# A hybrid attention and feed-forward block on one core: its opening staged by halves

## The chip, the core and the metric

The kernel runs on one core of a Trainium2 chip. The metric is the device time of one execution in microseconds (us). A profiled execution is shown beside three timed ones. Engines are named as the profile names them: PE is TensorE, DVE is VectorE, ACT is ScalarE, POOL is GpSimd, SP is SyncE. SP's queue of DMA instructions is SPq.

## The reference

For eight batches of 1024 tokens of width 256 (all float32):

```python
xn = layernorm(x)                                  # no gain, no bias
h  = silu(xn @ W1 + b1);  u, v, q, k = split(h, 4) # W1 is 256 x 1024
s  = silu(q_h @ k_h.T) / 1024                      # 16 heads of width 16
y  = (layernorm(concat(s @ v_h) * u) * gamma + beta) @ W2 + b2
f  = layernorm(xn) * ln1_g + ln1_b
f  = gelu(f @ ternary(w1).T + fb1)                 # hidden width 1024
f  = (layernorm(f) * ln2_g + ln2_b) @ ternary(w2).T + fb2
out = x + y + f
```

`ternary(w)` scales w by the mean of its absolute values, rounds to -1, 0 or 1 and scales back. That mean needs a sum over all of w before the first ternary weight exists.

## The kernel before

Tokens of a batch are laid out as 128 partitions by 8 tiles (T = 8) of 256 columns. Products that need more than the matmul's own precision are split: an operand is written as a rounded high part plus the rest as a low part, and three passes (high by high, high by low, low by high) are added up. So `W1h` and `W1l` are W1's parts, `xp` holds the two parts of the normalized and transposed x, and `kst` and `qst` hold two parts each of k and q.

The attention scores use heads in pairs with stacked parts: k and q parts are written from `kst` and `qst` to scratch in HBM (`write_parts`) and read back into `KS` and `QS` in a stacked layout (`load_k`, `load_q`). A transfer of one half h (512 tokens) and one parity o of the pairs has its own semaphore. PE's `scores(b, g)` waits for them; group g = 0 needs half 0 and o = 0 of both, g = 4 needs half 1 of `KS`.

Every engine walks the same list of steps. A step's name is `kind.args`: `ln1` (moments of x), `xn.i` (normalize the tile pair i), `xt.i` (PE transposes it, ACT writes the high part, DVE the low part), `k.c.h`, `q.c.h`, `v.i`, `u.c.h` (projections; ACT applies silu for k and q, DVE adds the bias for v), `vs.c` (ACT puts silu(v) into `V`), and those of the feed-forward part. Steps that go through PSUM take turns on the two banks of `fill`: the next step on a bank waits until the one before has been evacuated.

The list `OPENING` is what runs before the first scores, for batch 0. Each engine adds its own work around it. These are the places that the change touches or that the steps below speak of:

- SP (L475 to L490): loads x as one DMA, then `w1raw`, the two biases `b1s` and `bvb` (semaphore `s_b1`, full at 32), the feed-forward weights `wfraw` and `wsraw`, and small vectors. Then, for each half h: write k parts, write q parts, and for o = 0, 1 `load_k` and `load_q`.
- POOL (L500 to L546): constants and the identity, `input_rstd` (add eps, power -0.5, then the ratio of two such powers), and the zero fill of `V` (L546, 3072 columns).
- DVE (L891 to L899): moments of x, both parts of W1 whole (`split_w1`), a wait for `s_b1`, and the rest of `OPENING`.
- ACT (L625 to L634): the wait for `s_b1`, the list, and after each `q` step one sum of absolute values (`sum_of_abs`, L622), of `wfraw` after `q.0.0` and of `wsraw` after `q.0.1`. For k.0.1 it first waits until the first k parts have been written to HBM, for q.0.1 until the first q parts have.
- PE (L1088 to L1095): 36 warm-up matmuls, `xt.0`, `xt.1`, 8 warm-up matmuls, then `k.0.0` after `s_w1s`.

After the opening, the first rounds of scores carry the setup (`setup_step`): a total of the absolute sums on PE (L1047), scales and broadcasts and ternary weights on DVE (L669 to L695), products with them on PE (L1053 to L1069) and the folded biases on DVE (L701 to L711). Each engine takes its instructions in order, so a round of scores behind such a product waits for it.

## Time and profile before

| | |
|---|---|
| median of three executions | 1508.13 us (1507.6 to 1510.3) |
| the profiled execution | 1508.56 us, its span 1506.8 us |
| mean granted clock of the profiled execution | 0.994 |
| PE busy | 1465.9 us (97%) |
| ACT busy | 1205.8 us (80%) |
| DVE busy | 898.0 us (60%) |
| POOL busy | 97.4 us (6%) |
| first scores matmul starts | 39.73 us into the span |

The span is counted from the first to the last record of the execution; the execution's own time is 1.76 us longer. A time of day in the text below is one of the span. In a timeline row, the first figure is when a run of like instructions starts, the second how long it lasts, and the bracket how long the engine had been idle and who released it. A group of matmuls in full precision (f32) shows as two records for each instruction.

### The profile page before, as it was taken

What the parts mean: (1) busy time and instruction counts of PE and PEld (TensorE: products, weight loads), DVE (VectorE), ACT (ScalarE), POOL (GpSimd) and SP (SyncE); (2) the same over time, 40 slices, a digit from 0 to 9 for tenths busy, and PEclk for the clock granted to TensorE, in tenths of its full rate; (3) what the DMA queues carried; (4) which work ended last, traced back from release to release, by engine and by line L of the source; (5) the groups of instructions that cost most, each with busy time, mean ns of one, the idle gap of its engine ahead of it and who ended that gap; (6) DMA issues with size and microseconds to landing.
All of it is one profiled execution on the core that took longest, in us unless ns stands there. A gap on an engine that the chain in (4) does not pass through costs nothing.

```text
span 1506.8 us, 25898 instructions
## 1 busy us (share of the span) xinstructions
PE 1465.9 (97%) x9914; PEld 783.7 (52%) x9914; DVE 898.0 (60%) x1716; ACT 1205.8 (80%) x1269; POOL 97.4 (6%) x193
## 2 busy tenths in 40 slices
PE   7899999999999999999999999999999999999997
PEld 6354555455554555555555545545555455554544
DVE  5537664576555765458654685547765576555654
ACT  2688788888888887888878878788788888888884
POOL 2000100010000100001000010000100001000000
PEclk9899999999999999999999999999999999999999
DMA  6442043510524105241063401443033510425100
GB/s 202 110 128 69 1 102 96 140 57 16 126 68 129 57 15 154 76 103 47 17 167 89 122 1 54 129 128 83 1 94 103 140 57 15 119 66 138 29 1 29
DMA packets 67436, 123.49 MB, mean 82 GB/s; under 512 B 12784, under 2 KB 14448, under 8 KB 66288
## 3 DMA queue, kind: packets, MB, share of 16 engines
q1 hardware_dynamic: 67312, 121.83, 29.6%
q8 instruction: 79, 1.29, 0.4%
q14 instruction: 45, 0.37, 0.1%
HBM read 79.84 MB, written 41.94 MB: 81 GB/s over the span
## 4 chain that ended last, share of the span: by engine, by line
issue 93%; POOLq 6%; POOL 1%; DVE 0%; DVEq 0%
POOLq L534 3%; POOL rs L520 1%; POOLq L510 1%; POOLq L526 1%; POOLq L519 0%; POOLq L528 0%; POOLq L524 0%; POOLq L522 0%; POOLq L219 0%; DVE part L772 0%; DVEq L219 0%; POOL ident L500 0%; POOL rat L529 0%; POOLq L504 0%; POOLq L503 0%
## 5 line engine op out<-in xcount | busy, mean ns | idle before, releaser
L562 ACT ACTIVATE attn<-scores 128x1024 f32<-128x1024 f32 x1024 | 991.3, 1023 | 228.4 <-PE scores L930 224.3
L949 PE MATMUL outs<-attn,V 128*32 128x512 f32 x4096 | 494.3, 600 | 0.0
L930 PE MATMUL scores<-QS,KS 64*128 64x512 f32 x2048 | 389.1, 453 | 13.0 <-ACT attn L562 7.5
L930 PEld LDWEIGHTS scores<-QS,KS 64*128 64x128 f32 x2048 | 163.1, 185 | 306.2 <-ACT attn L562 241.5
L949 PEld LDWEIGHTS outs<-attn,V 128*32 128x32 f32 x4096 | 107.2, 109 | 235.7 <-issue 235.6
L822 DVE TENSOR_TENSOR tmp<-fill,l2g 128x512 f32<-128x512 f32 x128 | 88.5, 692 | 89.8 <-PE fill L1014 81.8
L805 DVE SCALAR_TENSOR_TENSOR hid<-fill,ratq,fb1b 128x512 f32<-128x512 f32 x128 | 96.1, 751 | 77.0 <-PE fill L1005 72.1
L1021 PE MATMUL fill<-Wq,hgh 128*128 128x256 f32 x512 | 130.2, 292 | 1.8 <-DVE hgl L829 1.1
L987 PE MATMUL fill<-xp,W1h 128*128 128x512 f32 x384 | 128.2, 415 | 0.0
L1021 PE MATMUL fill<-Wq,hgl 128*128 128x256 f32 x512 | 124.9, 282 | 0.0
L1021 PEld LDWEIGHTS fill<-Wq,hgh 128*128 128x128 f32 x512 | 97.3, 190 | 19.0 <-issue 14.9
L1021 PEld LDWEIGHTS fill<-Wq,hgl 128*128 128x128 f32 x512 | 97.6, 191 | 0.6
L509 POOL TENSOR_TENSOR rp<-mv,epst 128x2 f32<-128x2 f32 x64 | 12.5, 195 | 1316.4 <-DVE mv L722 911.2
L829 DVE TENSOR_TENSOR hgl<-tmp,hgh 128x512 fp32r<-128x512 f32 x128 | 88.6, 692 | 10.1 <-issue 0.4
L987 PEld LDWEIGHTS fill<-xp,W1h 128*128 128x128 f32 x384 | 66.1, 188 | 35.7 <-issue 25.6
L1014 PE MATMUL fill<-ident,hid 128*128 128x128 f32 x512 | 78.4, 281 | 3.5 <-DVE hid L805 2.1
L718 DVE BATCH_NORM_STATS2 st<-hid 128x6 f32<-128x512 f32 x128 | 79.1, 681 | 3.3 <-issue 0.5
L987 PE MATMUL fill<-xp,W1l 128*128 128x512 f32 x192 | 75.2, 392 | 0.0
L1014 PEld LDWEIGHTS fill<-ident,hid 128*128 128x128 f32 x512 | 56.0, 141 | 35.4 <-issue 25.7
L1005 PE MATMUL fill<-Wq,yT 128*128 128x512 f32 x256 | 71.6, 408 | 1.0
L1005 PE MATMUL fill<-Wq,yX 128*128 128x512 f32 x256 | 72.0, 410 | 0.0
L607 ACT ACTIVATE hid<-hid 128x2048 f32<-128x2048 f32 x32 | 60.4, 1911 | 7.7 <-DVE hid L805 7.5
(112 smaller groups left out, 1339.0 us busy)
## 6 DMA issues: line engine op xcount, KB each, us to landing
QS<-q_scratch SPq DMA_DIRECT2D x256, 128.0 KB, 3.2
k_scratch<-kst SPq DMA_DIRECT2D x64, 256.0 KB
q_scratch<-qst SPq DMA_DIRECT2D x64, 256.0 KB
KS<-k_scratch SPq DMA_DIRECT2D x128, 128.0 KB, 3.2
KS<-k_scratch SPq DMA_DIRECT2D x256, 64.0 KB, 3.4
xin<-in_x SPq DMA_DIRECT2D x8, 1024.0 KB, 5.0
out_dram<-part SPq DMA_DIRECT2D x16, 512.0 KB, 2.7
w1raw<-in_W SPq DMA_DIRECT2D x1, 1024.0 KB, 7.2
```

Source lines behind the costliest of these rows:

```text
L562: nc.scalar.activation(attn_of(g)[:, 2 * hf:2 * hf + 2, :], SP[:, 2 * hf:2 * hf + 2, :], ACT.Silu).then_inc(s_silu, 1)
L607: nc.scalar.activation(rows, rows, ACT.Gelu).then_inc(s_gelu, 1)
L718: V_.bn_stats(st[:, j, n, :] if len(views) > 1 else st[:, j, :], v)
L805: V_.scalar_tensor_tensor(out=hid_of(t)[:, cols], in0=FP[:, k, :], scalar=ratq[:, t:t + 1], in1=fb1b[:, cols], op0=ALU.mult, op1=ALU.add). ...
L822: V_.tensor_tensor(tmp[:, :].rearrange("p (c n) -> p c n", n=P), FP[:, k, :].rearrange("p (c n) -> p c n", n=P), l2g[:, 4 * r:4 * r + 4].u ...
L829: V_.tensor_tensor(hgl[:, r, :], tmp[:, :], hgh[:, r, :].bitcast(F32), ALU.subtract).then_inc(s_hg, 1)
L930: ins = mm(SP[:, j, :], KS[rows, pair, t * P:(t + 1) * P], QS[rows, pair - c * PPC, h * HALF:(h + 1) * HALF], start=True, stop=True)
L949: ins = mm(OP[32 * j:32 * j + 32, g // RUN % 2, :], V[:, t, c * HPC // 2 + j, o * DH:o * DH + 2 * DH], attn_of(g)[:, n, :], start=(o == 0 ...
L987: ins = mm(bank.rearrange("p (i n) -> p i n", i=2), w[:, kc, col:col + P], xp[:, 2 * h:2 * h + 2, part, kc, :], start=n == 0, stop=n == le ...
L1005: ins = mm(bank, y_of(t // 2)[:, part, kc, t % 2 * P:(t % 2 + 1) * P], Wq1[:, kc, hf * HALF:(hf + 1) * HALF], start=n == 0, stop=n == len( ...
L1014: ins = nc.tensor.transpose(bank[:, n * P:(n + 1) * P], hid_of(t)[:, col:col + P], ident[:, :])
L1021: ins = mm(bank[:, 0:D], w[:, r, n * P:(n + 1) * P], Wq2[:, 4 * r + n, :], start=i == 0, stop=i == len(passes) - 1)
```

## The change

x is loaded by two DMAs of four tiles each. For batch 0 the moments and the rstd are computed for four tiles at a time, with POOL's first power made on constants ahead of any data. `ln1` is now run inside the loop over `OPENING`, and so behind the wait for `s_b1`. The tile pair 1 of batch 0 is normalized into `tmp` instead of `normed`, so that it need not wait for the transposes of pair 0. W1 is split in four instructions instead of two: the high part of the columns of q and k after `xn.1`, their low part after `xt.1`, the high part of the columns of u and v after `xn.2`, their low part after `q.0.0`; `v.0` waits for that last one. `xt.1` and `xt.2` move ahead of `xn.2` and `xn.3`. The first 36 warm-up matmuls become 26. The load of QS for half 0 and o = 0 is issued by ACT, after `xt.3`, and no longer by SP; `sum_of_abs(0)` moves from behind `q.0.0` to behind `v.1`, which is ahead of `k.0.1`.

```diff
-WARM = (36, 8)
+WARM = (26, 8)
...
-OPENING = parsed("ln1 xn.0 xn.1 xt.0 xn.2 xt.1 k.0.0 q.0.0 xn.3 xt.2 v.0 xt.3 v.1 k.0.1 q.0.1 v.2 v.3 vs.0")
+OPENING = parsed("ln1 xn.0 xn.1 xt.0 xt.1 xn.2 k.0.0 q.0.0 xt.2 xn.3 v.0 xt.3 v.1 k.0.1 q.0.1 v.2 v.3 vs.0")
...
+        def normed_of(x, i):
+            return tmp[:, :].rearrange("p (j n) -> p j n", j=2) if (x, i) == (0, 1) else normed[:, :, :]
...
             def load_x(b):
-                sp.dma_start(xin[:, :, :], xv[b, :, :, :]).then_inc(s_x, 16)
+                for ts in (slice(0, T // 2), slice(T // 2, T)) if b == 0 else (slice(0, T),):
+                    sp.dma_start(xin[:, ts, :], xv[b, :, ts, :]).then_inc(s_x, 16)
...
                     load_k(0, 0, h, o)
-                    load_q(0, 0, h, o)
+                    if h or o:
+                        load_q(0, 0, h, o)
...
+            nc.gpsimd.tensor_tensor(rs1[:, 0:T // 2], epst[:, 0:T // 2], mhalf[:, 0:T // 2], ALU.pow)
...
+                for hf in range(2) if b == 0 else ():
+                    ts = slice(hf * T // 2, (hf + 1) * T // 2)
+                    pool.wait_ge(s_mv1, hf + 1)
+                    nc.gpsimd.tensor_tensor(rp1[:, ts], mv1[:, ts, 1], epst[:, ts], ALU.add)
+                    pool.drain()
+                    nc.gpsimd.tensor_tensor(rs1[:, ts], rp1[:, ts], mhalf[:, ts], ALU.pow).then_inc(s_rs1, 1)
...
+            def load_first_q():
+                act.wait_ge(s_qw, WROTE)
+                qv = qd[0].rearrange("(e w) r n -> e r w n", e=2)
+                for e in range(2):
+                    for at_row in (0, QROWS):
+                        act.dma_start(QS[e * TERMS + at_row:e * TERMS + at_row + QROWS, 0::2, 0:HALF].bitcast(F32),
+                                      qv[e, :, 0::2, 0:HALF]).then_inc(s_qst[0][0], 16)
...
                 step(0, *s)
-                if s[0] == "q":
-                    sum_of_abs(s[2])
+                if s == ("xt", NP - 1):
+                    load_first_q()
+                if s in (("v", 1), ("q", 0, 1)):
+                    sum_of_abs(int(s[0] == "q"))
...
-            step(0, "ln1")
-            split_w1(False)
-            dve.drain()
-            split_w1(True)
             dve.wait_ge(s_b1, 32)
             for s in OPENING:
-                if s != ("ln1",):
-                    step(0, *s)
+                step(0, *s)
+                if s == ("xn", 1):
+                    split_w1(0, 1)
+                elif s == ("xt", 1):
+                    split_w1(1, 1)
+                elif s == ("xn", 2):
+                    split_w1(0, 0)
+                elif s == ("q", 0, 0):
+                    split_w1(1, 0)
...
-                if s == [s for s in OPENING if s[0] in ("k", "q", "v")][0]:
+                if s == ("k", 0, 0):
                     warm_up(WARM[1])
                     pe.wait_ge(s_w1s, 1)
+                elif s == ("v", 0):
+                    pe.wait_ge(s_w1s, 2)
```

The order of instructions at two places of the opening follows, with the semaphores that each row waits for (`x_loaded` is `s_x`, `projection_biases_loaded` is `s_b1`, `w1_loaded` is `s_w1`, `input_rstd` is `s_rs1`; `filled` and `evacuated` are the two banks, `q_parts_written` is `s_qw`). DVE at the start of the program, before:

```order
L718 BN_STATS st_88<-xin 128x6 [waits x_loaded]
L718 BN_STATS st_88<-xin 128x6 x7
L722 BN_AGGR mv_89<-st_88 128x2 x8
L647 CAST W1h<-w1raw 128x2048 [waits w1_loaded]
L649 TENSOR_TENSOR W1l<-w1raw,W1h 128x2048
L732 TENSOR_SCALAR normed<-xin,mv_89,rs_91 128x256 [waits projection_biases_loaded,input_rstd]
L732 TENSOR_SCALAR normed<-xin,mv_89,rs_91 128x256
L732 TENSOR_SCALAR normed<-xin,mv_89,rs_91 128x256 [waits filled0]
```

The same place of the changed program:

```order
L746 BN_STATS st_88<-xin 128x6 [waits projection_biases_loaded,x_loaded]
L746 BN_STATS st_88<-xin 128x6 x3
L750 BN_AGGR mv_89<-st_88 128x2 x4
L746 BN_STATS st_88<-xin 128x6 [waits x_loaded]
L746 BN_STATS st_88<-xin 128x6 x3
L750 BN_AGGR mv_89<-st_88 128x2 x4
L760 TENSOR_SCALAR normed<-xin,mv_89,rs_91 128x256 [waits input_rstd]
L760 TENSOR_SCALAR normed<-xin,mv_89,rs_91 128x256
L760 TENSOR_SCALAR tmp<-xin,mv_89,rs_91 128x256 x2
L674 CAST W1h<-w1raw 128x2x512 [waits w1_loaded]
L882 TENSOR_TENSOR xp<-fill,xp 128x512 [waits x_high_part] x2
L677 TENSOR_TENSOR W1l<-w1raw,W1h 128x2x512
```

The wait for the biases has moved from the first normalization to the first statistics, W1's split from ahead of the normalizations to behind them, and both low parts of xp now stand ahead of pair 2. ACT from its first q step to the values for the first scores, before:

```order
L568 ACTIVATE qst<-fill,b1s 128x512 [waits filled1]
L622 ACTIVATE junk,asum<-wfraw 128x2048 [waits wf_loaded]
L588 ACTIVATE xp<-fill 128x512 [waits filled0] x2
L568 ACTIVATE kst<-fill,b1s 128x512 [waits filled0,k_parts_written]
L568 ACTIVATE qst<-fill,b1s 128x512 [waits filled1,q_parts_written]
L622 ACTIVATE junk,asum<-wsraw 128x2048 [waits abs_summed,ws_loaded]
L580 ACTIVATE V<-vraw 128x8x4x16 [waits evacuated1,pool_constants]
```

And now:

```order
L583 ACTIVATE qst<-fill,b1s 128x512 [waits filled1]
L603 ACTIVATE xp<-fill 128x512 [waits filled0] x2
L646 DMA QS<-q_scratch 32x2x512 [waits q_parts_written]
L646 DMA QS<-q_scratch 32x2x512 x3
L637 ACTIVATE junk,asum<-wfraw 128x2048 [waits wf_loaded]
L583 ACTIVATE kst<-fill,b1s 128x512 [waits filled0,k_parts_written]
L583 ACTIVATE qst<-fill,b1s 128x512 [waits filled1,q_parts_written]
L637 ACTIVATE junk,asum<-wsraw 128x2048 [waits abs_summed,ws_loaded]
L595 ACTIVATE V<-vraw 128x8x4x16 [waits evacuated1,pool_constants]
```

Four DMA issues that wait for the written q parts, and the sum over `wfraw`, now stand ahead of the activation of k.0.1, which before waited only for its product and the written k parts.

## Rows read from the trace of the kernel before

**Rows 1.** the page: busy time, share of the span and instructions by engine

```profile
PE 1465.9 (97%) x9914; PEld 783.7 (52%) x9914; DVE 898.0 (60%) x1716; ACT 1205.8 (80%) x1269; POOL 97.4 (6%) x193
```

**Rows 2.** timeline, 2 to 22 us: start us, us, engine line op out<-in xcount [idle before <-releaser]

```profile
2.15 0.71 SPq L478 DMA_DIRECT2D bvb<-in_b  x1
...
5.84 2.71 DVE L718 BATCH_NORM_STATS2 st<-xin 128x6 f32<-128x256 f32 x8 [4.84 <-DMA xin<-in_x]
...
8.62 0.64 DVE L722 BATCH_NORM_AGGREGATE mv<-st 128x2 f32<-128x6 f32 x8
...
10.45 2.29 DVE L649 TENSOR_TENSOR W1l<-w1raw,W1h 128x2048 fp32r<-128x2048 f32 x1
10.58 3.67 POOL L520 TENSOR_TENSOR rs<-rp,mhalf 128x8 f32<-128x8 f32 x1
...
14.29 0.74 DVE L732 TENSOR_SCALAR normed<-xin,mv,rs 128x256 f32<-128x256 f32 x2 [1.54 <-POOL rs L520]
...
17.02 1.12 PE L977 MATMUL fill<-ident,normed 128*128 128x128 f32 x4 [0.83 <-DVE normed L732]
...
17.31 2.66 POOL L546 MEMSET V<- 128x3072 f32 x1
...
17.93 3.62 PE L956 MATMUL scores<-ident 128*128 128x128 f32 x16
...
18.18 2.25 DVE L732 TENSOR_SCALAR normed<-xin,mv,rs 128x256 f32<-128x256 f32 x2 [0.43 <-PE fill L977]
...
21.36 0.80 PE L987 MATMUL fill<-xp,W1h 128*128 128x512 f32 x2
```

**Rows 3.** DMA issues of the first 16 us: KB each, us from issue to landing

```profile
bvb<-in_b SPq DMA_DIRECT2D x1, 128.0 KB, 8.5
```

**Rows 4.** group of POOL's 8-column power by shape: busy us, mean ns

```profile
L525 POOL TENSOR_TENSOR rs<-rp,mhalf 128x8 f32<-128x8 f32 x8 | 13.2, 1654 | 1.1
```

**Rows 5.** timeline, 25 to 41 us, columns as in rows 2

```profile
25.10 1.91 ACT L622 ACTIVATE junk<-wfraw 128x2048 f32<-128x2048 f32 x1
...
32.31 0.69 ACT L568 ACTIVATE kst<-fill,b1s 128x512 f32<-128x512 f32 x1 [2.67 <-PE fill L987]
...
33.41 0.40 PE L996 MATMUL fill<-W1h,xp 128*128 128x256 f32 x2
...
33.83 1.71 SPq L440 DMA_DIRECT2D QS<-q_scratch  x4
...
36.17 0.28 PE L996 MATMUL fill<-W1l,xp 128*128 128x256 f32 x1
...
37.82 1.15 ACT L580 ACTIVATE V<-vraw 128x512 f32<-128x512 f32 x2 [1.41 <-DVE vraw L862]
...
39.73 1.22 PE L930 MATMUL scores<-QS,KS 64*128 64x512 f32 x4 [3.28 <-DMA QS<-q_scratch]
40.56 3.85 ACT L562 ACTIVATE attn<-scores 128x1024 f32<-128x1024 f32 x4 [1.59 <-PE scores L930]
40.60 1.21 SPq L413 DMA_DIRECT2D k_scratch<-kst  x2
```

**Rows 6.** busy us in two stretches of time: PE, PEld, DVE, ACT, POOL, granted clock, DMA, GB/s

```profile
22.00:37.00 15.00, 12.57 (x79) 10.72 (x77) 8.67 (x15) 7.62 (x10) 0.00 (x0) 1.00 0.50 136
37.00:49.00 12.00, 8.47 (x32) 3.02 (x34) 5.48 (x21) 6.94 (x8) 0.00 (x0) 0.57 0.78 197
```

**Rows 7.** timeline, 43 to 63 us, columns as in rows 2

```profile
43.90 0.16 DVE L669 TENSOR_SCALAR cm<-outs 128x2 f32<-128x2 f32 x1 [6.17 <-PE outs L1047]
...
52.42 0.73 PE L930 MATMUL scores<-QS,KS 64*128 64x512 f32 x4 [0.97 <-DMA KS<-k_scratch]
...
56.60 1.23 DVE L682 TENSOR_SCALAR Wq<-wfraw 128x2048 fp32r<-128x2048 f32 x1
...
59.15 3.60 PE L1069 MATMUL fill<-Wq,bcasts 128*128 128x512 f32 x8
...
62.68 0.74 PE L930 MATMUL scores<-QS,KS 64*128 64x512 f32 x4
```

More of the change, by code:

```diff
@@ L513, in input_rstd @@
             def input_rstd(b):
-                pool.wait_ge(s_mv1, b + 1)
-                nc.gpsimd.tensor_tensor(rp1[:, 0:T], mv1[:, :, 1], epst[:, 0:T], ALU.add)
-                pool.drain()
-                nc.gpsimd.tensor_tensor(rs1[:, 0:T], rp1[:, 0:T], mhalf[:, 0:T], ALU.pow).then_inc(s_rs1, 1)
+                for hf in range(2) if b == 0 else ():
[4 more added lines that the diff above has]
+                    nc.gpsimd.tensor_tensor(rs1[:, ts], rp1[:, ts], mhalf[:, ts], ALU.pow).then_inc(s_rs1, 1)
+                if b:
+                    pool.wait_ge(s_mv1, b + 2)
+                if b:
+                    nc.gpsimd.tensor_tensor(rp1[:, 0:T], mv1[:, :, 1], epst[:, 0:T], ALU.add)
+                    pool.drain()
+                    nc.gpsimd.tensor_tensor(rs1[:, 0:T], rp1[:, 0:T], mhalf[:, 0:T], ALU.pow).then_inc(s_rs1, 1)
                 nc.gpsimd.tensor_tensor(rp1[:, T:2 * T], rp1[:, 0:T], epst[:, 0:T], ALU.mult)
@@ L641, in _, with split_w1 @@
             V_ = nc.vector
-            def split_w1(rest):
-                if not rest:
+            def split_w1(part, half):
+                cols = slice(half * 2 * D, (half + 1) * 2 * D)
+                if part == 0:
                     dve.wait_ge(s_w1, 16)
-                    V_.tensor_copy(W1h[:, :, :], w1raw[:, :, :])
+                    V_.tensor_copy(W1h[:, :, cols], w1raw[:, :, cols])
                 else:
-                    V_.tensor_tensor(W1l[:, :, :], w1raw[:, :, :], W1h[:, :, :].bitcast(F32),
+                    dve.drain()
+                    V_.tensor_tensor(W1l[:, :, cols], w1raw[:, :, cols], W1h[:, :, cols].bitcast(F32),
                                      ALU.subtract).then_inc(s_w1s, 1)
@@ L725, in norm_pair @@
             def norm_pair(x, i):
-                if i:
+                if i and (x, i) != (0, 1):
                     wait_filled(dve, x, ("xt", i - 1))
@@ L731, in norm_pair @@
                     t = 2 * i + j
-                    ins = V_.tensor_scalar(normed[:, j, :], xin[:, t, :], mv1[:, t, 0:1], rs1[:, t:t + 1],
+                    ins = V_.tensor_scalar(normed_of(x, i)[:, j, :], xin[:, t, :], mv1[:, t, 0:1], rs1[:, t:t + 1],
                                            ALU.subtract, ALU.mult)
@@ L835, in step @@
                 elif kind == "ln1":
-                    dve.wait_ge(s_x, 16 * (x + 1))
+                    if x == 0:
+                        for hf in range(2):
+                            dve.wait_ge(s_x, 16 * (hf + 1))
+                            ts = range(hf * T // 2, (hf + 1) * T // 2)
+                            stats([[xin[:, t, :]] for t in ts], st1[:, ts[0]:, :], mv1[:, ts[0]:, :], s_mv1)
+                        return
+                    dve.wait_ge(s_x, 16 * (x + 2))
                     stats([[xin[:, t, :]] for t in range(T)], st1, mv1, s_mv1)
@@ L840, in step @@
                     if i == 0:
-                        dve.wait_ge(s_rs1, x + 1)
+                        dve.wait_ge(s_rs1, x + 2 if x else 1)
+                    elif i == NP // 2 and x == 0:
+                        dve.wait_ge(s_rs1, 2)
                     norm_pair(x, i)
@@ L977, in step @@
                             ins = nc.tensor.transpose(bank[:, c * PAIR + j * P:c * PAIR + (j + 1) * P],
-                                                      normed[:, j, c * P:(c + 1) * P], ident[:, :])
+                                                      normed_of(x, i)[:, j, c * P:(c + 1) * P], ident[:, :])
                 elif kind in ("k", "q", "u"):
```

## The prediction, made before the changed kernel was run

> **What bounds the kernel now.** I read the page first, then the timeline of the first 63 us, then the DMA issues and the granted clock there. PE is busy for 97% of the span [rows 1], so a microsecond saved once, at the start, is one microsecond of the whole, and only where the next work on PE starts earlier. The change touches nothing after the opening, so the question is when PE comes to the group of scores behind the setup, the one that starts at 62.68 [rows 7]. From there on the two programs are the same, and I let the shift at that point stand to the end.
>
> Up to there three chains follow each other. In the first, x lands at 5.84, the moments take until 9.26, POOL's power until 14.25, DVE normalizes at 14.29, and PE starts k.0.0 at 21.36 [rows 2]. In the second, k and q go to HBM and back. SP issues the first QS loads, which wait for the written q parts, at 33.83, and PE then waits 3.28 us for QS, until 39.73 [rows 5]. In the third, ACT's first silu of scores starts at 40.56, and 22.1 us later, behind the setup, come the scores of 62.68 [rows 5, 7].
>
> **First chain.** DVE's first statistics now stand behind the wait for both biases. The later of them, bvb, is issued at 2.15 and lands 8.5 us later [rows 2, 3], at 10.65. Before, statistics started at 5.84, so the x halves (worth about half of x's transfer) have no one to serve. The statistics and aggregation of four tiles cost half of 2.71 and of 0.64 with a gap of 0.07 [rows 2], 1.75 us. The first moments are at 12.45, the second at about 14.3. POOL adds (no more than the 1.3 us that lay between moments and power before) and takes a power of four columns, between half and all of the 1.65 us of eight [rows 4]: first rstd at 13.3 to 15.4. I take the lower part, since the 1.3 us lay beside a DVE cast. DVE is itself busy until 14.3, so xn.0 starts at 14.3, against 14.29 before. Moments early, rstd in halves and the early power are thus worth nothing here: the late bias covers them.
>
> The first power before lasted 3.67 us, against 1.65 for a later one [rows 2, 4]. It ran beside DVE's low part of W1, which started at 10.45, lasted 2.29 and ended 1.5 us before the power did [rows 2]. By the Trainium skill, SBUF — State Buffer, section "SBUF: two separate sides", a DVE instruction with two SBUF inputs and a POOL instruction that reads SBUF exclude each other for a whole instruction. By that rule the 2 us were a blocked port and no first use of the power, and the early power would be worth nothing in any case; the sum does not need to decide it.
>
> Pair 1 has its own buffer, so its transposes follow those of pair 0 at once: 14.3 + 0.74 + two times 1.12 gives their end at 17.3, where it was 18.14 [rows 2]. The eight warm-up matmuls take 3.4 us (17.93 to 21.33) and then set k.0.0: 20.7 instead of 21.36. DVE's low part of W1's q and k columns, half of 2.29, is done by about 20 and does not bind. This is a gain of 0.7 us at most. Against it, the V fill of 2.66 us on POOL moves from 17.31 to somewhere at 19 to 20.5. Before, a normalization of 0.74 us that met it took 2.25 [rows 2]. Now it can meet xn.2 and the high part of the u and v columns, which stand ahead of k's parts on DVE: up to 0.7 us back. I take 0 for the first chain, with -0.7 and +0.7 as its ends. Behind q.0.0 the last quarter of the split (1.15 us) now delays v.0 by some 2 us; ACT's next wait covers that.
>
> **Second chain.** So the written q parts arrive at 33.8 as before. ACT now stands in front of k.0.1 waiting for them, issues four DMAs (on SP the same four took 1.71 us), sums wfraw (1.91 us), and only then activates k.0.1 [rows 5]: 33.8 + 1.7 + 1.9 = 37.4, against 32.31. That is 5.1 us late. PE cannot start v.2 before k.0.1 has left its bank, at 38.2. v.2 and v.3 are 24 matmuls that before ran right behind q.0.1, in 3.0 us (33.41 to 36.45 [rows 5]) at full clock (1.00 [rows 6]). DVE then empties the banks (1.4 us for both until ACT's 37.82, so 0.7 for the last) and ACT places V in 1.15. With a full clock ACT's first silu is at 38.2 + 3.0 + 0.7 + 1.15 = 43.1, which is 2.6 later than 40.56. But PE has then been idle for about 4 us, since the end of q.0.1's product. Before, it was idle for 3.28 us, and the mean clock of the stretch from 37 to 49 was 0.57 [rows 6]; at the lower of the two levels (1.2 GHz, half) all of v.2 and v.3 cost 3 us more. I take 1.7, since they are dense work that can win the clock back on the way: first silu at 44.8, 4.2 us late. QS lands before that (issued from 33.8 on, and it took until 39.73 before), so the wait of 3.28 us goes, but what stands in its place is longer.
>
> By the Trainium skill, DMA: Bandwidth & Descriptors, section "Issuing engines are not separate DMA queues", another issuing engine saves only issue time, which speaks against this move. The trace agrees: SP issued the first QS load at 33.83, the moment the parts had landed [rows 5], and had no issue time to save.
>
> **Third chain.** From the first silu to the scores of 62.68 were 22.1 us. 0.97 of them PE waited for the second half of KS [rows 7], whose parts SP wrote at 40.60, behind both QS issues [rows 5]. Now k.0.1's parts are ready at about 39.3 and SP is free, so this wait goes. The rest keeps: DVE's setup runs from 43.90 to 57.83 and is then 1.3 us ahead of the product at 59.15 that needs it [rows 7]. A faster PE could take up those 1.3 us and no more; I count half of them, 0.7, as what a full clock might give. I take 21.1: scores at 44.8 + 21.1 = 65.9, against 62.68.
>
> **The sum.** First chain 0, first silu +4.2, KS wait -1.0: +3.2 us on the profiled execution's 1508.56. The median of the runs shown lies 0.4 below that execution; on the median it is 1508.1 + 3.2 = 1511.3 us. Below: full clock for v.2 and v.3 (-1.7), the setup quicker (-0.7) and the first chain's -0.7 make +0.1. Above: all of them at the lower clock (+1.3), first chain +0.7 and DMA issues on ACT at twice SP's 1.71 us (+1.7; no row shows ACT issuing any) make +6.9.
>
> **The rivals.** *PE stays at or soon regains full clock* in v.2, v.3 and the first rounds: first silu 43.1, scores at 63.5 to 64.2, +0.8 to +1.5 us, so about 1509.3: not slower. For it speaks that v.2 and v.3 are dense and that the gap ahead of them, about 4 us, is little longer than the 3.3 us of before; against it, that the clock of before was low around that gap. It decides if v.2 and v.3 together take under 4 us.
> *The biases do not hold DVE.* If bvb landed by 6, or the wait did not stand where the order shows it, moments, rstd and transposes would move forward until ACT's own wait for b1 or W1's landing binds, k.0.0 would start near 14.5 and the written q parts be there 6.5 us sooner: 1508.1 + 3.2 - 6.5 = 1504.8 us. It breaks even if DVE is let go some 3 us earlier than 10.65. Against it stand 8.5 us in rows 3 and the order of instructions.
> *ACT's issues are slow and PE cold throughout:* issues of 3.4 us beside SP's KS loads, and the low clock, give +5 to +6.9, about 1514.
> *The change does not take effect:* that ACT's DMAs would be taken out of order with its activations, so that k.0.1 is not held; then only 0 to -0.7 is left, and 1508 us. Nothing in the profile shows an engine that does so.
>
> **How the numbers follow.** About 0.2% (3.0 us) is what a measurement of this kernel can tell from no change. Forecast 0.58 (+2.2 to +4.4; 0.36 of it beyond 3.0), full clock 0.18 (within), slow issues 0.14 (slower), no bias wait 0.06 (0.05 faster), no effect 0.04 (within). That gives slower 0.50, same 0.45, faster 0.05. The range from 1508.7 to 1514.0 leaves out the bias and no-effect cases and the outer edges of two others, some 2 in 10.
>
> **What would show it.** In the changed profile: DVE's first statistics at 10.7 behind bvb's landing; the first normalization at 14.3 to 14.7; k.0.0 at 20.7 to 21.4; four QS issues on ACT from 33.8; k.0.1's activation at about 37.4; no DMA wait ahead of the first scores, but vs.0 ahead of the first silu at 44 to 45; no KS wait ahead of the fifth group. The forecast is wrong if the statistics start near 5, if k.0.1's activation comes before 35, or if the scores behind the setup do not start later than 64.

## The result, and the profile after

| | before | after |
|---|---|---|
| median | 1509.43 us (1507.60 to 1510.36, 17 runs) | 1511.83 us (1511.12 to 1513.05, 17 runs) |
| ratio of the two | | 1.0020, 95% interval 1.0012 to 1.0027 |
| profiled execution | 1508.56 us, span 1506.8 | 1511.12 us, span 1509.3 |

The changed kernel is slower by about 2.4 us (1.8 to 4.1 by the interval), 0.2% of its time. The slowest of the 17 runs of before is faster than the fastest of the 17 of after. PE's busy time is the same but for 0.4 us [rows 1]; the first line of the page of after:

```profile
PE 1466.3 (97%) x9894; PEld 783.6 (52%) x9894; DVE 899.0 (60%) x1718; ACT 1205.6 (80%) x1269; POOL 97.1 (6%) x196
```

The first chain in the timeline of after (columns as in [rows 2]; a row with x2 groups neighbours, and its length is from the first's start to the last's end):

```profile
10.54 1.41 DVE L746 BATCH_NORM_STATS2 st<-xin 128x6 f32<-128x256 f32 x4 [9.54 <-DMA bvb<-in_b]
...
12.82 1.01 POOL L529 TENSOR_TENSOR rs<-rp,mhalf 128x4 f32<-128x4 f32 x1
...
14.24 0.74 DVE L760 TENSOR_SCALAR normed<-xin,mv,rs 128x256 f32<-128x256 f32 x2
...
18.45 1.22 DVE L677 TENSOR_TENSOR W1l<-w1raw,W1h 128x1024 fp32r<-128x1024 f32 x1
18.73 1.00 POOL L544 TENSOR_TENSOR rat<-rat,rp 128x8 f32<-128x8 f32 x1
19.68 2.66 POOL L561 MEMSET V<- 128x3072 f32 x1
...
19.84 2.96 DVE L760 TENSOR_SCALAR normed<-xin,mv,rs 128x256 f32<-128x256 f32 x2 [0.17 <-issue]
...
21.42 0.69 ACT L583 ACTIVATE kst<-fill,b1s 128x512 f32<-128x512 f32 x1 [3.79 <-PE fill L1026]
...
23.48 0.43 DVE L888 CAST kst<-kst 128x512 fp32r<-128x512 f32 x1
```

These rows show that DVE stands until 10.54 behind the bias bvb (9.54 us idle, released by its DMA), that rstd comes in halves of 1.01, and that the first normalization starts at 14.24, where it was 14.29 [rows 2]. ACT's k.0.0 comes at 21.42, but the cast that has to follow it on DVE only at 23.48: between them stand xn.2, which takes 2.96 us beside POOL's fill of V, and a cast of W1's high part. k.0.0 starts on PE at 19.74, 1.6 us earlier than the 21.36 of before [rows 2], and its parts are cast only 0.4 us earlier (23.48 against 23.84): nearly all that the transposes moved forward won is lost there.

The second chain, the same view (SPq and ACTq are the DMA queues of SyncE and ScalarE):

```profile
30.36 5.55 SPq L431 DMA_DIRECT2D KS<-k_scratch  x12
...
33.41 1.78 ACTq L646 DMA_DIRECT2D QS<-q_scratch  x4
...
35.24 1.91 ACT L637 ACTIVATE junk<-wfraw 128x2048 f32<-128x2048 f32 x1 [3.49 <-issue]
...
37.15 0.67 ACT L583 ACTIVATE kst<-fill,b1s 128x512 f32<-128x512 f32 x1
...
37.87 0.51 PE L1035 MATMUL fill<-W1h,xp 128*128 128x256 f32 x2 [1.50 <-ACT kst L583]
...
40.73 0.28 PE L1035 MATMUL fill<-W1l,xp 128*128 128x256 f32 x1
...
42.00 0.73 PE L969 MATMUL scores<-QS,KS 64*128 64x512 f32 x4 [0.99 <-DMA QS<-q_scratch]
42.00 1.15 ACT L595 ACTIVATE V<-vraw 128x512 f32<-128x512 f32 x2 [1.71 <-DVE vraw L898]
43.05 1.92 ACT L577 ACTIVATE attn<-scores 128x1024 f32<-128x1024 f32 x2
```

ACT issues the four QS loads at 33.41, for 1.78 us, sums wfraw for 1.91 and comes to k.0.1 at 37.15, where it was 32.31 [rows 5]. PE starts v.2 at 37.87, after 1.50 us without work, and ends v.3 at 41.01, 3.1 us, at the clock of before. QS lands only now: PE waits 0.99 us for it and scores from 42.00. The first silu of scores starts at 43.05, behind V; it was at 40.56 [rows 5], so 2.5 us later.

The third chain:

```profile
53.25 0.73 PE L969 MATMUL scores<-QS,KS 64*128 64x512 f32 x4
...
63.51 0.74 PE L969 MATMUL scores<-QS,KS 64*128 64x512 f32 x4
```

The scores of the fifth group start at 53.25 with no wait for KS (before 52.42 behind 0.97 us of it [rows 7]), and those behind the setup at 63.51, against 62.68: the shift is down to +0.83. By the end of the span it is 2.5 us (1509.3 less 1506.8). The 1.7 us between come all at once, at 74 to 77.4 us, where neither the text of the kernel nor the order of its instructions differs:

```profile
22.00:37.00 15.00, 10.41 (x48) 8.57 (x46) 8.37 (x14) 3.75 (x5) 0.34 (x1) 0.77 0.53 137
37.00:49.00 12.00, 7.83 (x46) 4.80 (x50) 6.60 (x23) 10.00 (x14) 0.00 (x0) 0.90 0.82 202
72.00:74.00 2.00, 1.11 (x8) 0.53 (x12) 0.00 (x0) 2.00 (x3) 0.00 (x0) 1.00 0.00 0
74.00:76.00 2.00, 2.00 (x12) 0.43 (x8) 0.00 (x0) 1.17 (x2) 0.00 (x0) 0.50 0.00 0
76.00:78.00 2.00, 2.00 (x13) 0.38 (x5) 0.00 (x0) 0.14 (x1) 0.00 (x0) 0.65 0.00 0
```

(Columns as in [rows 6].) In the stretches up to 49 the clock is 0.77 and 0.90, where it was 1.00 and 0.57 [rows 6]: the low clock lay beside v.0 and v.1 (26.2 to 33.0) and not beside v.2 and v.3. From 49 to 74 it is 1.00 again but for the last moments of a low stretch that ends at 50.1, then 0.50, the lower of its two levels (1.2 and 2.4 GHz), and from 77.4 on 1.00. The profiled execution of before is at 1.00 there. Sixteen products of attn and V, which take 1.92 us at the full clock, take 3.52 here, 1.6 us more, and nothing later gives that back. Their row in the timeline of after:

```profile
73.81 3.52 PE L988 MATMUL outs<-attn,V 128*32 128x512 f32 x16
```

**A second profile of each kernel** shows how far such falls are a matter of the single execution:

> The changed kernel once more, one profile. If the fall of PE's clock ten microseconds behind the setup is a matter of the execution, this one may lack it or have it elsewhere; what is of the kernel (first statistics 10.5 to 11, k.0.1's activation 37.1 to 37.5, QS's landing behind 41) stays. The scores behind the setup come at 63.5 where PE's clock is full in v.2 and v.3, and up to 66 where it is not.

> The kernel before once more, one profile. Its first profile has the scores behind the setup at 62.68 and no fall of the clock after 49. If its upper group of times (about 1509.9) are executions with a later or longer fall, a profile with an execution time above 1509 shows one, or a later arrival at those scores; a profile below 1508.7 shows none.

They took 1511.39 and 1512.43 us (one execution each). Of the second profile of after, the timeline:

```profile
37.74 0.50 PE L1035 MATMUL fill<-W1h,xp 128*128 128x256 f32 x2 [2.52 <-ACT kst L583]
...
42.09 0.27 PE L1035 MATMUL fill<-W1l,xp 128*128 128x256 f32 x1
...
43.18 1.15 ACT L595 ACTIVATE V<-vraw 128x512 f32<-128x512 f32 x2 [3.03 <-DVE vraw L898]
44.24 1.92 ACT L577 ACTIVATE attn<-scores 128x1024 f32<-128x1024 f32 x2
```

Here v.2 and v.3 are the 4.6 us from 37.74 to 42.36, 1.5 us more than in the first profile, because the clock is low from 38.6 to 42.0. The first silu is at 44.24, the scores behind the setup at 65.23 (+2.55), and no fall comes after them. The second profile of before has two falls, the rows of 70 and of 76 us:

```profile
70.00:72.00 2.00, 2.00 (x12) 0.22 (x4) 0.00 (x0) 1.34 (x2) 0.00 (x0) 0.50 0.00 0
...
76.00:78.00 2.00, 2.00 (x16) 0.31 (x8) 0.00 (x0) 0.79 (x1) 0.00 (x0) 0.50 0.00 0
```

Its scores behind the setup come at 63.47, 0.79 later than in the first profile, and the two falls cost 1.67 and 1.61 more. So each of these three stretches behind the setup, where PE is the bound, cost about 1.6 us, before has such stretches too, and two profiles of one kernel can differ by more than the two kernels do. Profiles tell what each step does; what the change is worth is told by the medians. Of the two profiles of after, each has lost time to such stretches, the second in v.2 and v.3 and in the first rounds (45.4 to 52.2), the first at 74.

The mean granted clock of whole executions is 0.990 to 0.993 in the 17 of after and 0.992 to 0.997 in the 53 of before that ran beside the experiments, so after does spend more time at the lower clock. That is not all of the difference: with the same mean of 0.992, 7 executions of after took 1511.1 to 1513.0 us and 13 of before 1508.0 to 1510.8.

### The profile page after: what moved, and what is told of

Read it like the earlier page. It is cut to its first block, busy times and chain, and to the rows that moved or that the text cites. A ratio compares the mean times of both kernels' runs of the same rounds, so it can differ in the third digit from the quotient of the medians.

```text
span 1509.3 us, 25869 instructions
## 1 busy us (share of the span) xinstructions
PE 1466.3 (97%) x9894; PEld 783.6 (52%) x9894; DVE 899.0 (60%) x1718; ACT 1205.6 (80%) x1269; POOL 97.1 (6%) x196
## 4 chain that ended last, share of the span: by engine, by line
issue 93%; POOLq 6%; POOL 1%; DVE 0%; DVEq 0%
POOLq L549 3%; POOLq L517 1%; POOLq L541 1%; POOL rs L535 1%; POOLq L539 0%; POOL rs L529 0%; POOLq L543 0%; POOLq L534 0%; POOLq L537 0%; POOL rat L544 0%; POOLq L219 0%; DVE part L800 0%; POOLq L528 0%; DVEq L219 0%; POOL ident L510 0%
## 5 line engine op out<-in xcount | busy, mean ns | idle before, releaser
L1053 PE MATMUL fill<-ident,hid 128*128 128x128 f32 x512 | 78.5, 281 | 3.0 <-DVE hid L833 2.1
L888 DVE CAST kst<-kst 128x512 fp32r<-128x512 f32 x32 | 13.7, 427 | 89.5 <-ACT kst L583 89.4
```

The source lines that it names most:

```text
L1053: ins = nc.tensor.transpose(bank[:, n * P:(n + 1) * P], hid_of(t)[:, col:col + P], ident[:, :])
```

## The experiments

Each group of experiments ran beside its own runs of before, whose medians were 1508.99 (first four: e1, e2, e4, e5), 1509.28 (e3, e6, e7, e8) and 1508.47 us (e9, e10 and the two profiles above). Line numbers in fences of experiments are those of their own kernels.

My theory had two parts: the new wait for the biases makes everything in front of k.0.0 worthless, and the ACT part (first QS half issued on ACT, sum over wfraw in front of k.0.1) is what costs. Rivals: that the front is worth nothing for another reason (POOL, W1's landing, PE's warm-up), and that the loss comes from PE's clock and not from either.

### e1_bias_late: the biases waited for where they are used

```diff
+                if s == ("v", 0):
+                    dve.wait_ge(s_b1, 32)
                 step(0, *s)
...
+                if s == ("k", 0, 0):
+                    act.wait_ge(s_b1, 32)
...
-                            dve.wait_ge(s_x, 16 * (hf + 1))
+                            dve.wait_ge(s_x2 if hf else s_x, 16)
```

The waits ahead of the two loops go; x's second half gets a semaphore of its own, s_x2, since the shared count would let the first half's wait pass on parts of both.

> The changed kernel, with DVE's wait for the biases moved behind to v.0, ACT's to k.0.0, and a semaphore of its own for the second half of x (without one, a wait for the first half could be met by the second). Theory A (bvb's landing at 10.5 sets DVE's first statistics, and that cancels all gains of the first chain): statistics start near 5, the first normalization near 8, k.0.0 near 13 instead of 19.6, the written q parts near 26.5 instead of 33.4, and the whole is 5 to 7 us below the changed kernel, 3 to 5 below the one before. Rival B (W1's landing or the load of the queue binds anyway): k.0.0 not earlier than 17, gain under 3 us.

Measured: 1506.01 us (1505.45 to 1506.91, 11 runs), ratio 0.9984 (0.9975 to 0.9992).

```profile
4.82 1.41 DVE L748 BATCH_NORM_STATS2 st<-xin 128x6 f32<-128x256 f32 x4 [3.83 <-DMA xin<-in_x]
...
8.53 0.73 DVE L762 TENSOR_SCALAR normed<-xin,mv,rs 128x256 f32<-128x256 f32 x2
...
16.12 0.69 ACT L584 ACTIVATE kst<-fill,b1s 128x512 f32<-128x512 f32 x1 [4.15 <-PE fill L1029]
```

Statistics start at 4.82, with half of x, against 5.84 before [rows 2] and 10.54 in after; the first normalization at 8.53, k.0.0's activation at 16.12 instead of 21.42. On PE k.0.0 starts at 14.36, later than the 13 that I expected, since the low part of W1 now comes last (1.29 us of waiting for it). So the bias wait did cover the front, and without it halves and early moments are worth some 5 us: the medians against their own before are +2.4 with the wait and -3.0 without. In its profile the scores behind the setup are 4.45 us earlier than in before's, and a fall of the clock at 68.7 to 72.1 takes 1.65 of them back.

### e2_q_on_sp: after without the ACT part

```diff
-                    if h or o:
-                        load_q(0, 0, h, o)
+                    load_q(0, 0, h, o)
...
-                if s == ("xt", NP - 1):
-                    load_first_q()
-                if s in (("v", 1), ("q", 0, 1)):
-                    sum_of_abs(int(s[0] == "q"))
+                if s[0] == "q":
+                    sum_of_abs(s[2])
```

> The changed kernel with its ACT part undone: first QS load on SP again, the sum over wfraw behind q.0.0 again. Theory A (ACT held in front of k.0.1 costs 2.5 us at the first silu and 0.8 at the setup, net of the KS wait that it takes away): k.0.1's activation at 32 to 33, first silu at 40.0 to 40.5, scores behind the setup at 62.3 to 62.7, so 0.8 to 1.2 earlier than in the changed kernel. Theory C (the other 1.7 us are a fall of PE's clock at about 74, a matter of how the idle times fall in a given execution): total within 0.7 us of the kernel before where there is no such fall, up to 2 above where there is. Rival: the rest of the change costs it, then the scores behind the setup stay at 63.5.

Measured: 1508.37 us (1507.34 to 1509.93, 11 runs), ratio 0.9998 (0.9989 to 1.0007): no difference from before.

The two rows of ACT in its timeline:

```profile
35.84 0.69 ACT L582 ACTIVATE kst<-fill,b1s 128x512 f32<-128x512 f32 x1 [3.36 <-PE fill L1023]
...
41.84 1.92 ACT L576 ACTIVATE attn<-scores 128x1024 f32<-128x1024 f32 x2
```

k.0.1's activation is 1.3 us earlier than in after but 3.5 later than the 32.31 of before, and the scores behind the setup are at 63.19, where I expected 62.3 to 62.7 and after has 63.51. The steps of my theory were wrong here; only its total, within 0.7 us of before, came out. What I had overlooked: v.0 waits for the last quarter of W1's split, behind q.0.0, and v.0, v.1 and k.0.1 then run at a lower clock (27.0 to 33.8). I had let ACT's next wait cover that; it does in after only, where ACT does not come to k.0.1 before 37.15 anyway. That the late split costs what its early q and k columns won is my reading of these rows; no run undoes the late split in this kernel.

### e5_only_act: before with the ACT part alone

The edit of e2 the other way round, put into before, with load_first_q() as in the change.

> The kernel before with the ACT part alone: first QS load on ACT after xt.3, the sum over wfraw behind v.1. Theory A: ACT waits for the written q parts until 33.8, k.0.1's activation at 37.4, first silu at 43.3, setup's scores near 63.6, 0.8 to 1.2 us above before; the KS wait ahead of the fifth group is gone. Rival (the rest of the change is what costs): first silu at 40.6 and no change.

Measured: 1513.46 us (1512.04 to 1514.13, 5 runs), ratio 1.0033 (1.0020 to 1.0045). k.0.1's activation is at 37.12 and the first silu at 44.22, 3.7 later than before; behind the setup +1.97 is left, and a fall of the clock at 75.1 to 78.5 makes +3.6 of it. The cost is well above the 0.8 to 1.2 us that I expected. PE stands idle for 4.86 us ahead of v.2 here, the clock is at its lower level from 37.6 to 41.0, and most of v.2 and v.3 runs in it. By the medians the ACT part alone (+4.5) costs more than the whole change (+2.4), as if the rest of the change, which alone is worth nothing (e2), made up for some of it; the two intervals overlap.

### e4_late_and_sp: both undone

> Both: biases waited for late, x's second half on its own semaphore, and the ACT part undone. Theory A: the first chain's gain of 5 to 7 us arrives whole, and none of it is given back on ACT: 5 to 8 us below the kernel before, the fastest of these four. Rival: the wfraw and wsraw loads (until about 19) now meet the k and q writes, the sums or the setup become late, and the gain stays under 4 us.

Measured: 1501.98 us (1500.85 to 1503.38, 5 runs), ratio 0.9958 (0.9946 to 0.9971). The first silu is at 34.31, 6.2 us earlier than before, and the scores behind the setup are 6.3 earlier. The ACT part thus costs 4.0 us with late biases (e1 less e4, by medians of one group), 3.0 with early ones (after at +2.4 against e2 at -0.6) and 4.5 on before. In the profiles of the same three pairs it costs less at the scores behind the setup, 1.9, 0.3 and 2.0 us; in each pair the kernel with the ACT part then has a fall of the clock of 1.6 to 1.7 us behind the setup and the other has none. Whether the ACT part brings these falls on is open: the second profile of before has two, the second of after none.

What still holds the front back is one collision:

```profile
13.73 3.30 DVE L759 TENSOR_SCALAR normed<-xin,mv,rs 128x256 f32<-128x256 f32 x2 [0.17 <-issue]
...
13.90 2.67 POOL L561 MEMSET V<- 128x3072 f32 x1
...
17.70 0.43 DVE L887 CAST kst<-kst 128x512 fp32r<-128x512 f32 x1
```

xn.2 takes 3.30 us for its two tiles, which alone take 0.74, because POOL fills V meanwhile, and k.0.0's cast comes at 17.70, 2.35 us after its activation at 15.35.

### e3_abs_back: after, the sum over wfraw behind q.0.0 again

```diff
-                if s in (("v", 1), ("q", 0, 1)):
-                    sum_of_abs(int(s[0] == "q"))
+                if s[0] == "q":
+                    sum_of_abs(s[2])
```

> The changed kernel with the sum over wfraw back behind q.0.0, the QS load still on ACT. Of the hold in front of k.0.1 (from 32.5, when its product is done, to 37.15), 1.9 us are that sum: theory A expects k.0.1's activation at 35.2, first silu at 41.1 to 41.6 and the scores behind the setup at 62.6 to 63.0, if the second half of KS does not bind first. Rival (QS's landing, at 42.0 in the changed kernel, binds): first silu not before 43.0 and nothing gained.

Measured: 1510.60 us (1509.66 to 1511.63, 10 runs), ratio 1.0006 (0.9997 to 1.0015); against its own before +1.3, which the interval does not tell from nothing, where after has +2.4. k.0.1's activation is at 35.48, 1.7 earlier than in after, as expected, but the first silu only 0.5 earlier:

```profile
40.35 1.15 ACT L595 ACTIVATE V<-vraw 128x512 f32<-128x512 f32 x2 [1.71 <-DVE vraw L898]
...
41.73 1.22 PE L969 MATMUL scores<-QS,KS 64*128 64x512 f32 x4 [2.37 <-DMA QS<-q_scratch]
42.57 1.94 ACT L577 ACTIVATE attn<-scores 128x1024 f32<-128x1024 f32 x2 [1.07 <-PE scores L969]
...
64.11 0.73 PE L969 MATMUL scores<-QS,KS 64*128 64x512 f32 x4
```

V is in place at 41.5, and PE waits 2.37 us for QS, which lands at 41.7, 0.3 earlier than in after. Behind the 1.9 us of the sum stands the landing of QS. The scores behind the setup come at 64.11, later than the 63.51 of after and than the 62.6 to 63.0 expected: the clock is at its lower level from 41.7 to 51.9 here, in after's first rounds only from 46.7 to 50.1. No run moves the sum and leaves the load on SP, so the two halves of the ACT part are told apart by this run alone.

QS lands late with the load on the second queue. The issues of these few us in after:

```profile
QS<-q_scratch ACTq DMA_DIRECT2D x4, 128.0 KB, 5.4
KS<-k_scratch SPq DMA_DIRECT2D x2, 128.0 KB, 5.0
```

and the same view of before, for the QS loads that its SP issued at 33.83:

```profile
QS<-q_scratch SPq DMA_DIRECT2D x4, 128.0 KB, 3.3
KS<-k_scratch SPq DMA_DIRECT2D x1, 128.0 KB, 3.7
```

(KB each, median us from issue to landing.) With SP free of the QS loads, its twelve KS loads all go out from 30.36 on, and ACT's four share the transfers with them: 5.4 us for each where it took 3.3, and 5.0 for a KS load beside them where it took 3.7. All profiled kernels agree: 5.0 to 5.4 us where ACT issues (after twice, e1, e3, e5, e7), 3.0 to 3.4 where SP does (before twice, e2, e4, e6, e8, e9, e10). So PE has QS 2.3 us later (42.0 against 39.73) although its issues began 0.4 us earlier. By the Trainium skill, DMA: Bandwidth & Descriptors, section "Issuing engines are not separate DMA queues", loads run on the same 16 engines and interleave, whoever issues them. The trace agrees: both sets of loads became slower together, and the issue time saved does not pay for it. No run has ACT's four loads in flight by themselves, so a share of that queue's own is not excluded.

### e6_only_power: before with the early power alone

```diff
+            nc.gpsimd.tensor_tensor(rs1[:, 0:T // 2], epst[:, 0:T // 2], mhalf[:, 0:T // 2], ALU.pow)
```

> The kernel before with the early power alone. Theory P (the long first power, 3.67 us, waits for a port that DVE holds during the low part of W1, as the add before it waits for DVE's cast): the early power takes 1.0 us, the first add stays at 1.1 and the first real power at 3.7, and nothing moves. Rival (first use costs 2 us): the early power takes 3 us, the real one 1.6, and the first normalization moves from 14.3 to about 12.8, when W1's split ends.

Measured: 1509.38 us (one execution).

```profile
1.59 1.02 POOL L506 TENSOR_TENSOR rs<-epst,mhalf 128x4 f32<-128x4 f32 x1
...
9.09 1.09 POOL L519 TENSOR_TENSOR rp<-mv,epst 128x8 f32<-128x8 f32 x1 [6.48 <-DVE mv L723]
10.20 2.29 DVE L650 TENSOR_TENSOR W1l<-w1raw,W1h 128x2048 fp32r<-128x2048 f32 x1
10.32 3.67 POOL L521 TENSOR_TENSOR rs<-rp,mhalf 128x8 f32<-128x8 f32 x1
...
14.64 1.65 POOL L526 TENSOR_TENSOR rs<-rp,mhalf 128x8 f32<-128x8 f32 x1
```

The first normalization starts at 14.02, as much earlier than in before as the statistics do (5.58 against 5.84). The power that is the first of the program takes 1.02 us, no more than the later ones of four columns (1.01). The one at 10.32 takes 3.67 us as before, although it is no longer the first: it is held while DVE's low part of W1 (two SBUF inputs) runs, from 10.20 to 12.49, and 3.67 is about that rest (2.17) plus 1.65. The early power is worth nothing, and there is no first use to pay for. By the Trainium skill, SBUF — State Buffer, section "SBUF: two separate sides", a DVE instruction with two SBUF inputs and a POOL instruction that reads SBUF exclude each other for a whole instruction. The trace agrees. DVE's cast of W1, which has one input (8.93 to 10.13), held POOL too: the add at 9.09 ends about when the cast does and takes 1.09 us, where elsewhere it takes 0.20.

### e7_after_filled and e8_before_filled: does work for PE in the gaps keep its clock up?

```diff
+                    if b == 0 and 3 <= n <= 5:
+                        pe.wait_ge(s_setup, 4)
+                        for _ in range(2):
+                            mm(FP[:, 1, 0:P], ident[:, :], ident[:, :], start=True, stop=True)
```

Both kernels get six products more than the reference asks for, whose results nobody reads, in the rounds in which falls had been seen.

> The changed kernel with two full-size matmuls on the identity behind the first scores of rounds 3, 4 and 5 of batch 0 (six in all, 1.4 us of PE time, in a stretch where PE waits for ACT). They compute nothing that is used. Theory C (1.66 of the 2.5 us are PE's clock at its lower level from 74.0 to 77.4): no lower clock there, and the median 1 to 1.7 us under the changed kernel's 1511.8. Rival (the lower clock is an accident of the profiled execution and the 2.4 us have another cause): same or up to 1.4 us slower.

> The kernel before with the same six matmuls. Its times fall into two groups, near 1507.8 and near 1509.9. Theory C (the upper group are executions with that fall of the clock): the upper group disappears, all runs near 1508, median about 1 us lower. Rival (the two groups have another cause, or the fillers push the scores): two groups as before, or all 0.5 to 1.4 us slower.

Measured: e7 1516.15 us (1513.42 to 1518.03, 6 runs), ratio 1.0047 (1.0033 to 1.0060); e8 1511.90 (1510.66 to 1514.15, 12 runs), ratio 1.0019 (1.0011 to 1.0028). My expectation was wrong in both. e7's profile has no fall there, but each pair of fillers pushes the scores behind it, by 2.2 us in all; its median is 4.5 us further above its own before than after's is, and the rest of that is not explained. e8's has one all the same, which before's first profile had not:

```profile
76.00:78.00 2.00, 2.00 (x10) 0.37 (x4) 0.00 (x0) 0.00 (x0) 0.00 (x0) 0.50 0.00 0
```

The filling is itself too dear to tell what it does for the clock. What e8 does show, as the second profile of before does, is that a fall there does not need the ACT part: neither has any of it. What sets the place of a fall stays open.

### e9_v_first and e10_v_first_uv_now: what e4 left

e9 is e4 with POOL's fill of V ahead of everything that waits for x; e10 is e9 with the low part of the u and v columns right behind their high part.

```diff
-            pool.wait_ge(s_const, 2)
+            nc.gpsimd.memset(V[:, :, :, :], 0.0).then_inc(s_const, 1)
+            pool.wait_ge(s_const, 3)
             step(0, "ln1")
-            nc.gpsimd.memset(V[:, :, :, :], 0.0).then_inc(s_const, 1)
```

```diff
                 elif s == ("xn", 2):
                     split_w1(0, 0)
+                    split_w1(1, 0)
-                elif s == ("q", 0, 0):
-                    split_w1(1, 0)
```

> The late-bias and SP kernel of before (1502.0), with POOL's zero fill of V moved ahead of the moments, where POOL is idle until 7. Theory P (the fill blocks DVE's normalization of pair 2 for its whole length): that pair takes 0.74 instead of 3.3 us, k's parts are split 1.0 to 1.5 us earlier, and the whole gains about as much. Rival (k.0.0's product or the clock sets the parts): nothing moves.

> The same, and the low part of the u and v columns of W1 right behind their high part, so ahead of k's parts on DVE. It costs the k and q parts up to 0.5 us and takes away PE's wait of 3.5 us ahead of v.0, which also lets the clock fall to its lower level; v.0 starts near 17 instead of 21. Expected: k.0.1's activation 3 to 6 us earlier, but QS's landing then sets the first scores, so 0.5 to 2 us below the kernel with the V fill alone; 1498.5 to 1501 in all. Rival: the k and q parts being later costs as much as it gives.

Measured: e9 1500.83 us (1500.46 to 1502.92, 4 runs), ratio 0.9949 (0.9935 to 0.9962); e10 1502.82 (1500.66 to 1504.34, 5 runs), ratio 0.9959 (0.9945 to 0.9973). Both beat both kernels; between them the runs don't decide (spans 1498.9 and 1499.1). e10's median lies above the 1498.5 to 1501 that I expected. The timeline of e9, first the opening and then the first scores:

```profile
2.57 2.66 POOL L559 MEMSET V<- 128x3072 f32 x1
...
14.30 0.74 DVE L759 TENSOR_SCALAR normed<-xin,mv,rs 128x256 f32<-128x256 f32 x2 [0.17 <-issue]
...
16.66 0.43 DVE L887 CAST kst<-kst 128x512 fp32r<-128x512 f32 x1 [1.03 <-ACT kst L583]
```

and

```profile
32.81 0.73 PE L969 MATMUL scores<-QS,KS 64*128 64x512 f32 x4 [1.25 <-DMA QS<-q_scratch]
...
33.44 2.92 ACT L577 ACTIVATE attn<-scores 128x1024 f32<-128x1024 f32 x3
```

The fill runs while everybody waits for x, xn.2 is back at 0.74 us, and the cast of k comes 0.7 after its activation. The scores behind the setup are 7.7 us earlier than before's, 1.4 more than e4's; by medians against their own before e9 gains 7.6 us and e4 7.0. In e10 PE starts v.0 at 17.33 instead of 20.53, and its first silu is at 32.73 instead of 33.44, but that changes next to nothing behind the setup (-7.86 against -7.74 from before). In between, PE waits in both for the second half of KS ahead of the fifth group (0.65 us until 44.67 in e9, 0.47 until 44.55 in e10), and there the lead of 0.7 is gone: in these profiles the next bound is that second half's way through HBM, not v.0.

## Why the prediction was right

Its time, 1511.3 us, is 0.5 from the median, and the main causes held: the bias covers the front, and ACT's two jobs ahead of k.0.1 make the kernel slower. That the number is so close is partly luck. It stands on the median of three runs, 1508.1, where the 17 gave 1509.4; the shift put on it was +3.2, and +2.4 was measured. And one term was paid at another place than foreseen, since a stretch at the lower clock came behind the setup and not ahead of it.

- **First chain, 0.** Right, and for its reason. Statistics were foreseen at 10.65 and came at 10.54; xn.0 foreseen at 14.3, came at 14.24. The first moments were worked out as 12.45, where 10.65 and 1.75 make 12.40; they came at 12.40. k.0.0 was put at 20.7 to 21.4 and started at 19.74, a gain of 1.6 us where I allowed 0.7 at most. All but 0.4 of it was given back at xn.2 (2.96 us beside the fill) and the cast behind it, where I allowed 0.7: both terms measured about twice what I gave them, and they cancelled. The written q parts were expected at 33.8 and were there at 33.41 or earlier. e1 shows that it was the bias: with that wait gone the same front is 5 us quicker, and the rival of the biases had its numbers right (k.0.0 at 14.36 for 14.5, the written q parts 6.56 us earlier for 6.5, the whole 3.0 below before for 3.3).
- **The early power, nothing.** Right; e6 shows it alone.
- **Second chain, k.0.1 at 37.4.** It came at 37.15: 1.78 us of issues and 1.91 of the sum, as foreseen. e3 shows the sum's share, e2 and e5 the whole.
- **v.2 and v.3 at a lower clock, +1.7.** Wrong in the profile shown: 3.1 us at the full clock, and the first silu at 43.05, the number of the first rival. In the second profile they took 4.6 (+1.5), and the silu came at 44.24, against 44.8 foreseen. I had treated as a fixed term what falls differently from one execution to the next. The idle time that I took as its reason was also too long: not about 4 us, but 1.50 in the first profile and 2.52 in the second. The late split had put v.0 at 27.33 instead of 25.25 and the lower clock had slowed v.0 and v.1, so q.0.1's product ended at 36.37, where before it ended at 33.58. In e5, without the late split, the idle time was 4.86 us and the clock was low from 37.6. That the shorter idle time kept the clock up is argued from these rows and not tested.
- **"QS lands before that".** Wrong. It landed at 42.0, 8.6 us after the first issue, where before it took 5.9 [rows 5]. I took the old duration for a queue that had not been there, beside KS loads that would now all be ahead. It cost nothing only because V was placed at the same moment (silu at 43.05); e3 shows it as the next bound.
- **Third chain, KS wait -1.0.** Right: 53.25 without a wait. I took 21.1 us from the first silu to the scores; it took 20.5 in the first profile and 21.0 in the second. "Scores behind the setup not before 64" was therefore missed in the first (63.51), by which the prediction's own sign calls the forecast wrong, and met in the second (65.23, foreseen 65.9).
- **"From there the two programs are the same, and I let the shift stand to the end."** This step failed. The instructions are the same, but in the first profile the clock fell at 74.0 and added 1.7 us. +3.2 was foreseen, +0.83 stood at 63 us and +2.5 at the end. The clock's price of about 1.7 was right, its place was not, and I had not allowed for a fall behind the setup, which before's first profile did not show.
- **Late split of the u and v columns, "ACT's next wait covers that".** Right for this change, but it is, as I read the rows, why e2 is no better than before: the cover goes when the ACT part goes.

The first rival had its mechanism right for one profile (full clock in v.2 and v.3, +0.8) and its total wrong: no run of after came under 1511.1. That no execution was as quick as 1509.3 argues that a stretch at the lower clock is paid somewhere nearly always; it was not shown why.

## What to carry to other kernels

A wait set once ahead of a loop costs nothing as long as what it waits for is there first; when the work behind it is made earlier, the wait becomes the bound and hides the gain. Look at every wait in front of the moved work, and put it where its data is used. An engine in the critical chain should not be the one that waits for a written scratch and issues its reload: the wait stands in front of its own work, and here a second queue went with later landings while both queues had transfers in flight (5.4 us for 3.3). Compare medians when the effect is about 2 us of 1500, and use profiles for the steps.

## What the runs showed of the hardware that I had not expected

- Loads of 128 KB in flight on two queues at once took 5.0 to 5.4 us each (medians, in after), where one queue's took 3.3 to 3.7 (before).
- A fill of 2.66 us on POOL, which reads nothing, held DVE's normalization: 2.96 and 3.30 us for two tiles instead of 0.74. The other way round, DVE's cast and its difference of two SBUF inputs held POOL: 1.09 and 1.00 us (after, 18.73) for operations that take 0.20, 3.67 for a power of 1.65. DVE's statistics did not hold POOL (12.32 to 13.69 beside a power of 1.01).
- The clock fell to its lower level in places that differ from one execution of a kernel to the next (38.6 and 74.0 in two profiles of after, nowhere behind the setup and at 69.1 and 75.9 in two of before). Ahead of the fall at 74.0 PE had waited for ACT 0.54 and 0.41 us between groups of scores; in before's first profile it waited exactly as long at 71.6 and 72.6, and the clock stayed at its upper level. Each fall behind the setup cost 1.6 to 1.7 us.
